# Softmax sums inverted once per row in a compact tile, and spread over the partitions by DMA

## The reference

```python
h = h + _L0_attn_ref(_layernorm(h), kernel, head_kernel)
h = h + _L0_ffn_ref(_layernorm(h), ...)

# attention, of which the change touches the softmax
scores = jnp.einsum('bhsk,bhtk->bhst', q, k) / jnp.sqrt(K)
probs = jax.nn.softmax(scores, axis=-1)
o = jnp.einsum('bhst,bhtk->bhsk', probs, v)
```

## Time and profile before

| | |
|---|---|
| median of 3 runs | 5212.7 us (5208.45 to 5214.74) |
| span of the profiled execution | 5214.6 us |
| PE matmul busy | 4965.0 us (95%) |
| PE weight load busy | 3227.2 us (62%) |
| DVE busy | 3832.6 us (73%) |
| POOL busy | 2796.0 us (54%) |
| ACT busy | 2665.8 us (51%) |
| DVE reciprocals of `sums` | 543.1 us, 768 of them |
| mean granted PE clock | 0.980 |

### The profile page before, as it was taken

One profiled execution on the slowest core, in us unless ns is written; L12 is line 12 of the kernel. 1 busy time (PEld: TensorE's weight loads), 2 busy tenths in 40 slices (PEclk: granted clock), 3 DMA queues, 4 the chain that ended last, 5 costly groups with the idle time before them and its releaser, 6 DMA issues. The chain is left out here.

```text
span 5214.6 us, 92843 instructions
## 1 busy us (share of the span) xinstructions
PE 4965.0 (95%) x25829; PEld 3227.2 (62%) x25829; DVE 3832.6 (73%) x8495; ACT 2665.8 (51%) x6408; POOL 2796.0 (54%) x1611
## 2 busy tenths in 40 slices
PE   5999999999999999999999999999999999999997
PEld 3556666666566666666666666666666656666666
DVE  5667768677776777777777776777867777677765
ACT  2664555555544545545455455455455554554542
POOL 0665555555555555555555555555555555555652
PEclk7999999999999999999999999999999999999998
DMA  1000000000000000000000000000000000000000
GB/s 39 6 10 7 6 16 6 11 7 6 16 6 10 7 10 11 6 11 11 10 6 6 10 11 11 7 6 16 6 11 7 6 16 6 10 6 10 6 1 14
DMA packets 43025, 49.54 MB, mean 10 GB/s; under 512 B 26256, under 2 KB 34311, under 8 KB 42503
## 3 DMA queue, kind: packets, MB, share of 16 engines
q1 hardware_dynamic: 42503, 43.12, 2.7%
HBM read 23.45 MB, written 19.09 MB: 8 GB/s over the span
## 5 line engine op out<-in xcount | busy, mean ns | idle before, releaser
L1155 POOL TENSOR_TENSOR sums<-sums,probs 128x736 f32<-128x736 f32 (+3 forms) x1344 | 2384.6, 1774 | 1278.0 <-ACT probs L867 1262.6
L867 ACT ACTIVATE probs<-scores 128x368 f32<-128x368 f32 (+3 forms) x3456 | 1460.1, 474 | 1922.0 <-PE scores L761 1814.5
L925 DVE TENSOR_REDUCE part_max<-work 128x1 f32<-128x368 f32 (+3 forms) x3456 | 1657.3, 527 | 310.1 <-PE work L675 288.3
L778 PE MATMUL o_ps<-probs,values 128*64 128x368 f32 (+1 forms) x6912 | 1455.7, 500 | 0.0
L759 PE MATMUL scores<-q_a,k_a 128*128 128x368 f32 (+3 forms) x3456 | 1170.2, 339 | 61.1 <-issue 41.5
L761 PE MATMUL scores<-q_b,k_b 128*128 128x368 f32 (+3 forms) x3456 | 1146.4, 332 | 0.0
L675 PE MATMUL work<-k_a,q_a 128*128 128x368 f32 (+3 forms) x3456 | 1089.6, 378 | 48.0 <-DVE part_max L925 24.4
L675 PEld LDWEIGHTS work<-k_a,q_a 128*128 128x128 f32 (+1 forms) x3456 | 578.3, 184 | 777.4 <-issue 624.1
L1151 POOL TENSOR_TENSOR sums<-probs 128x736 f32<-128x736 f32 (+1 forms) x192 | 343.6, 1789 | 863.5 <-ACT probs L867 861.5
L759 PEld LDWEIGHTS scores<-q_a,k_a 128*128 128x128 f32 (+1 forms) x3456 | 639.5, 185 | 83.8 <-issue 33.2
L761 PEld LDWEIGHTS scores<-q_b,k_b 128*128 128x128 f32 (+1 forms) x3456 | 641.3, 186 | 53.0 <-issue 33.7
(11 more groups left out here) (186 smaller groups left out, 5039.6 us busy)
## 6 DMA issues: line engine op xcount, KB each, us to landing
resid_rows<-h_in SPq DMA_DIRECT2D x16, 576.0 KB, 2.8
h_out<-resid_rows SPq DMA_DIRECT2D x16, 576.0 KB, 4.1
h_in<-in_pe_table_dram SPq DMA_DIRECT2D x16, 512.0 KB
out_dram<-h_out SPq DMA_DIRECT2D x16, 512.0 KB
q_b<-max_rows SPq DMA_DIRECT2D x128, 4.0 KB
q_b<-max_rows SPq DMA_DIRECT2D x128, 0.3 KB
counts<-in_x_dram SPq DMA_DIRECT2D x16, 116.0 KB, 3.0
out_raw<-n_expert_out_weight_dram SPq DMA_DIRECT2D x1, 1024.0 KB
```

What stands on the lines that cost most here:

```text
L778: mm = nc.tensor.matmul(o_ps[64 * i:64 * i + 64, 0:cw], values[0:n, t, h * DH:(h + 1) * DH], probs[0:n, s % NP, i, 0:cw], start=(t == 0), ...
L867: nc.scalar.activation(probs[0:n, s % NP, i, 0:cw], scores[0:n, h % SB, 0:cw], ACT.Exp, scale=DH ** -0.5).then_inc(probs_ready, 1)
L925: nc.vector.tensor_reduce(part_max[0:n, i * NT + j, c:c + 1], w[0:n, 0:keys], AX.X, ALU.max).then_inc(drained[k], 1)
L1155: nc.gpsimd.tensor_tensor(acc, acc, probs[0:n, s % NP, :, 0:cw], ALU.add).then_inc(sums_done, 1)
```

## The change

The unit `sum` stays. At its own step SP, once ACT's copy has landed, now takes one row of each half of `sums` and lays it out as `row_sums`, 92 partitions by 8 columns, with two DMAs. Three steps after (TURN_ROUND) DVE inverts this small tile into `row_inverse`; SP writes it to DRAM, waits for that, and reads it back with two DMAs, each of which repeats a row of 368 over 64 partitions of `sums`. Five steps after (SCALE), the step at which it stood before, DVE multiplies `heads_t`; it now waits for these two DMAs. The planner counts one `invert` of 20 at the third step, in place of 63 at each of four steps.

```diff
-DIV = 4
+TURN_ROUND, SCALE = 3, 5
+SLICES, SLICE = 92, 8
-JOB = {"invert": 63, "scale": 45, "split": 50, ...
+JOB = {"invert": 20, "scale": 45, "split": 50, ...
         if u[0] == "sum":
-            for part in range(DIV):
-                job(s + 1 + part, "invert")
-            job(s + 1 + DIV, "scale")
+            job(s + TURN_ROUND, "invert")
+            job(s + SCALE, "scale")
...
+    inverse_dram = nc.dram_tensor("inverse_rows", (2, CHUNK), F32, kind="Internal").ap()
+    row_sums = sb(ctx, "row_sums", [SLICES, SLICE])
+    row_inverse = sb(ctx, "row_inverse", [SLICES, SLICE])
...
     # DVE
-        def divide(seg, it, b, q, part):
-            ...
-            inverse = sums[:, q % 2, 0, :]
-            if part == 0:
-                wait_drained(dve, seg, it, ("sum", q))
-            if part < DIV:
-                cols = slice(part * CHUNK // DIV, min((part + 1) * CHUNK // DIV, cw))
-                nc.vector.reciprocal(inverse[:, cols], inverse[:, cols]).then_inc(s_chain, 1)
-            else:
-                dve.wait_ge(s_chain, inverted[q])
-                dve.wait_ge(heads_out, n + 1)
-                o = heads_t[:, q // NC, c0:c0 + cw]
-                nc.vector.tensor_tensor(o, inverse[:, 0:cw], o, ALU.mult).then_inc(heads_scaled, 1)
+        def invert(b, q):
+            dve.wait_ge(sums_spread, 32 * (item_of(b, q) + 1))
+            nc.vector.reciprocal(row_inverse[:], row_sums[:]).then_inc(sums_inverted, 1)
+
+        def divide(b, q):
+            n = item_of(b, q)
+            c0, cw = CHUNKS[q % NC]
+            dve.wait_ge(inverse_back, 32 * (n + 1))
+            dve.wait_ge(heads_out, n + 1)
+            o = heads_t[:, q // NC, c0:c0 + cw]
+            nc.vector.tensor_tensor(o, sums[:, q % 2, 0, 0:cw], o, ALU.mult).then_inc(heads_scaled, 1)
...
     # DVE's step, after the units of step s
+            for u in seg.at[s - TURN_ROUND] if s >= TURN_ROUND else []:
+                if u[0] == "sum":
+                    invert(b, u[1])
+            for u in seg.at[s - SCALE] if s >= SCALE else []:
+                if u[0] == "sum":
+                    divide(b, u[1])
...
     # SP's step
+            for u in seg.at[s - TURN_ROUND] if s >= TURN_ROUND else []:
+                if u[0] == "sum":
+                    n = PAIRS * NC * (b - 1 if u[1] == PAIRS * NC - 1 else b) + u[1]
+                    wait_then(sp.wait_ge, sums_inverted, n + 1)
+                    sp.dma_start(inverse_dram.rearrange("a (p n) -> (a p) n", n=SLICE), row_inverse[:]).then_inc(inverse_out, 16)
+                    wait_then(sp.wait_ge, inverse_out, 16 * (n + 1))
+                    for i in range(2):
+                        sp.dma_start(sums[64 * i:64 * i + 64, u[1] % 2, 0, :],
+                                     inverse_dram[i:i + 1, :].broadcast_to((64, CHUNK))).then_inc(inverse_back, 16)
             for u in seg.at[s]:
+                if u[0] == "sum":
+                    wait_then(wait_drained, sp, seg, it, u)
+                    for i in range(2):
+                        sp.dma_start(row_sums[i * SLICES // 2:(i + 1) * SLICES // 2, :],
+                                     sums[64 * i:64 * i + 1, u[1] % 2, 0, :].rearrange("a (p n) -> a p n", n=SLICE)).then_inc(sums_spread, 16)
                 if u[0] == "maxrow":
```

More of the change, by code:

```diff
@@ L83 @@
 STEP = (130, 0, 70)
-JOB = {"invert": 63, "scale": 45, "split": 50, "statistics": 90, "moments": 130, "rank": 200, "weights": 200}
+JOB = {"invert": 20, "scale": 45, "split": 50, "statistics": 90, "moments": 130, "rank": 200, "weights": 200}
 EVEN_MAX, EVEN_V, EVEN_POST = (0, 1, 0), (1, 0, 0), (1, 0.5, 0)
@@ L563, in fusion_kernel @@
     heads_scaled = sem("heads_scaled")
+    sums_spread = sem("sums_spread")
+    sums_inverted = sem("sums_inverted")
+    inverse_out = sem("inverse_out")
+    inverse_back = sem("inverse_back")
     qk_hi = sem("qk_hi")
@@ L892, in _ @@
         done = [0]
-        inverted = {}
         def then(ins):
@@ L979, in unit, with item_of @@
                 nc.vector.tensor_tensor(o, w, o, ALU.add).then_inc(drained[k], 1)
[L981 to L997 removed]
+        def item_of(b, q):
+            return PAIRS * NC * (b - 1 if q == PAIRS * NC - 1 else b) + q
+        def invert(b, q):
[3 more added lines that the diff above has]
+            n = item_of(b, q)
+            c0, cw = CHUNKS[q % NC]
+            dve.wait_ge(inverse_back, 32 * (n + 1))
+            dve.wait_ge(heads_out, n + 1)
+            o = heads_t[:, q // NC, c0:c0 + cw]
+            nc.vector.tensor_tensor(o, sums[:, q % 2, 0, 0:cw], o, ALU.mult).then_inc(heads_scaled, 1)
         def split_flat(seg, it, c):
@@ L1082, in step @@
                 unit(seg, it, b, u)
-            for part in range(DIV + 1):
-                for u in seg.at[s - 1 - part] if s > part else []:
-                    if u[0] == "sum":
-                        divide(seg, it, b, u[1], part)
+            for u in seg.at[s - TURN_ROUND] if s >= TURN_ROUND else []:
[4 more added lines that the diff above has]
+                    divide(b, u[1])
             if seg.post:
```

3 lines of the change are left out of this document (removed).

## The result

| | before | after |
|---|---|---|
| median of 4 runs each | 5210.8 us (5208.4 to 5214.7) | 5280.4 us (5271.3 to 5293.0) |
| ratio, 95% interval | 1 | 1.0133 (1.0118 to 1.0149) |
| span of the profiled execution | 5214.6 us | 5268.9 us |
| mean granted PE clock | 0.980 | 0.978 |

The changed kernel is 70 us slower; 5196 us and a range up to 5250 us were predicted. The profiled execution of the changed kernel is the fastest of its four and that of the kernel before the slowest of its four, so the traces show 54 us of the 70.

What follows compares the result with a forecast made beforehand. PE, busy 95% of a 5214.6 us span, was taken as the bound. A gain of 58 us against costs of 25 + 5 + 5 + 5 gave -18 us, so 5196 us, with a range from 5148 to 5250.

Steps and rivals of the forecast that it cites:

- The gain: PE's waits for DVE shrink as reciprocals go: 58 us saved, bounds 30 and 95 us.
- The scale on DVE: DVE's multiplication of heads_t now waits for the broadcasts, holding up drains behind it: 5 us cost, bounds 0 and 40.
- The row of maxima: Loads of maxima into q_b queue on SP behind the inverse's DRAM trip: 25 us, plus 5 edges and 5 clock.
- rival 3: DVE stands at the heads_t scale in most of 192 sums if broadcasts land after 4.1 us: 5235 us, chance 0.06.
- the lateness: Delay of q_b's maxima loads from inversion, DRAM write and two broadcast issues: 3.2 us, bounds 2.6 and 4.7.
- The second pair: Step 50: maxima 6.5 us late against 4.9 us slack, behind an expert unit; 1.7 us stall per image.
- the first: First pair, step 23: maxima 0.8 us late, but PE pays this or the leftover counts wait; cost 0.1 us per image.
- The fourth: Fourth pair, step 104, loop's end: PE waits for ACT anyway, slack 2.9 plus some 1.3 us, so no stall.
- The clock: A PE stall of the size expected at the row of maxima may lower the granted clock: 5 us cost.
- (a): PE's 1.55 us wait for counts at 2360.98: 0.85 us saved per image, as POOL sets the ranking's end.
- (b): PE's 1.37 us wait at 2380.92, two reciprocals ahead of it: 1.2 us saved per image.
- (c): PE's 1.42 us wait at 2387.29, four reciprocals ahead of it: 1.1 us saved per image.

Runs made afterwards that it cites:

- 9: Changed kernel with DVE multiplying heads_t six steps after the sum instead of five, SP's order unchanged: 5249.8 us, ratio 1.0083.
- 5: Changed kernel with SP's loads of the row of maxima ahead of the inverse's DRAM round trip, and heads_t multiplied six steps after the sum: 5183.7 us, ratio 0.9950.
- 3: Changed kernel with SP's loads of the row of maxima first and units placed by the old costs: 5233.7 us, ratio 1.0043.
- 6: Changed kernel with loads of the row of maxima first, units placed by the old costs, heads_t multiplied six steps after the sum: 5168.0 us, ratio 0.9918.
- 11: Kernel before with one reciprocal of eight columns replacing four of 92, no DMA added, units placed by the new costs: 5195.8 us, ratio 0.9974.
- 4: Kernel before with one reciprocal of eight columns replacing four of 92, no DMA added, old placement: 5175.0 us, ratio 0.9935.
- 1: Changed kernel with SP's loads of the row of maxima ahead of the inverse's DRAM round trip in the same step: 5229.1 us, ratio 1.0036.
- 8: Changed kernel with SP's load of h_out set at step 1 instead of step 0: 5283.5 us, ratio 1.0137.
- 2: Changed kernel with units placed by the old costs, 63 at each of four steps: 5305.1 us, ratio 1.0181.
- experiment 7: Kernel before with the DRAM round trip's DMAs added on SP, using tiles of their own that DVE never waits for: 5316.1 us, ratio 1.0200.

## Why the prediction was wrong

Three steps of the prediction failed, each with a number from the runs. The gain was set at 58 us and measured 14 under the placement that the change brings: the relief alone is worth 35 and not 58, and the new placement costs 21 of these again, which the sum had at nothing without a reason. The scale on DVE was set at 5 us and measured 30 to 66. The row of maxima was set at 35 us and measured 51.

**The heads' scale on DVE.** It was sized at 5 us with a bound of 40, and it measured 30 in the changed kernel (9), 45 behind the loads of maxima (5) and 66 in the old placement (3 to 6). The chain was right: broadcasts in 2.7 us, from the inversion to the scale 4.9 us at the least, against 5.6 predicted. Wrong was the sentence that four banks of PE hide 1 us of standing. Apart from the loop's end, DVE stands for 1.2 us or more at only one sum of most images, but there the 1.2 us are followed by a multiplication of 1.58 us and statistics before the next drain. PE's wait is 0.94 us and step 64 takes 1.2 us more, and with no broadcast to wait for there is neither (11). This is the place of rival 3, to which 0.06 was given, but not its condition: it asked for broadcasts that land after 4.1 us and for a wait in most sums, and they land after 2.7 us. The multiplication's length belongs to it: in 5 it is 1.22 us at that place, and its mean falls from 993 ns in the changed kernel to 782 ns in 5 and 666 ns in 6. How much of the 30 to 66 us is the standing and how much the longer multiplication was not separated.

**The row of maxima: the lateness was right, the whole term came out larger.** The lateness came out as 2.9 to 3.1 us where 3.2 was summed, and 6.3 where 6.5 was; the way out took 1.48 us, not 2.0, and lies below the 1.8 to 2.3 us that were to be seen, while the two issues took 1.15 us and not 0.9. (The Trainium skill, "DMA: Bandwidth & Descriptors", section "Anatomy of one DMA — SWDGE (gpsimd) path", has about 2.0 us fixed on its path; this store, issued by SP, is below it.) The second pair stalls for 1.5 us (1.7 predicted). At the first, PE was to pay one of two waits, 0.8 us for the maxima or 0.7 left over of `counts`, and it pays 0.8 us for the maxima in twelve images of fourteen, where 4 leaves 0.79 of `counts`: this was right. The fourth was put at no stall, since ACT was idle there for 3.86 us. PE's idle time at step 0 grows by 1.3 us an image, but by 1.5 without the DMAs (11), so how much of it is the row of maxima stays open; putting the loads first gives 0.8 us back (1). Why the second group of scores waits 4.2 us in the rows shown instead of 2.5 stays open too; 8 was meant to test it and did not. The first image took 12 us longer and the last 7, where 5 were set for both, and moving the loads first gives back 8 in the first and nothing in the last. The clock, set at 5 us, was not small where the stall at the second pair was longer: by the estimate there, it is nearly all of the 49 us of busy time in 2. So the term measured 51 us by experiment 1, against 25 + 5 + 5 = 35 predicted.

**The gain of 58 us was 35 (4), and with the new placement 14 (11).** By 4, the relief took 0.76 us of (a) in the eight images whose clock does not fall at step 23 (1.55 to 0.79 us), where 0.85 was predicted, and 1.34 us of (b), where 1.2 was, but only 0.2 us of (c), where 1.1 was. In the other six images of 4 the wait of (a) is gone, but the steps 20 to 27 take 21.6 us there against 21.0, so that is no gain. It is the new placement that takes (c) away, in 11 and in the changed kernel. What failed is the reading of the planner: it was used only where it helped. The same cheaper `invert` sets PE waiting at steps 4, 57, 58, 85 and 104 for other drains, 2.7 us an image, which uses up the 2.7 us that it takes away at the steps 18, 35, 83, 84, 90 and 99; and PE's idle time at step 0 grows by 1.6 us. Together that is the 21 us by 4 and 11. The orders of the engines held the moves of the drains, and only the stretches around the old stalls were read; for step 0 the trace shows no releaser.

The 0.79 us left of (a) bear out the reading that POOL sets the end of the ranking. In the loop's images of 4 that still wait, its last instruction takes 1.73 us and ends 0.04 us after POOL's; it takes 0.18 us in those where the clock fell at step 23, and PE does not wait. In 4, shortest, median and longest in ns:

```profile
L1047 DVE TENSOR_SCALAR rank<-rank x16: 182/958/1734, 440.5 to 5103.3; 128x36 f32<-128x36 f32 x16
```

**The terms were added as if they were apart.** They share DVE's queue and SP's: loads first makes the scale stand for longer (257 us against 162), the new placement also shortens the second pair's stall (1.5 us against 2.3), and the turn-round a step earlier removes more than the 70 us. A sum of 58, 25 and 5 with signs of their own could not show that. Two small slips of the sum change nothing: the lower bound of the lateness is 0.2 + 1.6 + 0.1 + 0.8 = 2.7 us, not 2.6, and two thirds of 0.42 with rival 1 make 0.46 for faster, not 0.49.

What was to be seen and was: L711's wait nearly gone, the waits of steps 33 to 36 gone, `q_b` by 1.5 us at the second pair. What was to be seen and was not: a way out of 1.8 to 2.3 us, DVE at 3330 us (it is 3438; the `max` drains alone are busy for 1697.5 us against 1657.3 before), and a single pair that waits. The prediction named two of its failures ahead: `q_b` waits in three places, and `heads_t` for its broadcast by more than 1 us, though in 49 of the 192 sums and not in most.

## What to carry to other kernels

An instruction that waits at the head of an in-order queue costs by what stands behind it, not by how often it waits: ask of each new wait which drain comes next, and whether it can be put behind that drain (one step later here: 30 to 66 us). A blocking round trip on a queue that also carries loads on the path belongs behind them, in the same step. And a planner fed with new costs is a change of its own: time the relief with the old placement first (here 35 us against 14). And add up idle and busy time of the engine that bounds: an entry in the list of waits may only have taken the place of another (experiment 7), and a loss may not be idle time at all (experiment 2).

## What the runs showed of the chip that was not expected

- A store of 2.9 KB to DRAM that SP waits for lets SP's next DMA out 1.48 us after its own issue, 1.22 us after that issue's 0.26 us. That is shorter than the 1.6 us from issue to landing of the smallest load in the earlier trace rows.
- A reciprocal of 92x8 takes 187 ns, one of 128x92 713 ns: 526 ns for 84 columns, 6.3 ns each.
- The multiplication of `heads_t` with the same shape takes 666 to 1142 ns on average, by kernel: 666 ns in 6, 1142 ns in 3, which differ only in the step in which it stands.
- PE's same 25829 matmuls are busy for 4953.6 us in 11 and 5035.0 us in 2, at mean granted clocks of 0.981 and 0.968.
